# First attention: 32-row scores in two row groups, values of two units in four column groups of one bank, the inputs of the values behind the first scores

## The reference, cut to what matters

```python
qkv = x @ qkv_w + qkv_b                       # 8 heads of 8 channels
attn = einsum('bijnd,bijnpqd->bijnpq', q * hd**-0.5, kn) + bias   # a 7x7 neighbourhood
a = softmax(attn)
out = einsum('bijnpq,bijnpqd->bijnd', a, vn) @ proj_w + proj_b
gate = sigmoid(relu(x @ g1_w + g1_b) @ g2_w + g2_b)
y = x + out * gate                            # then a layer norm
```

## Time and profile before

| | us |
|---|---|
| median of 3 runs | 428.79 (427.92 to 429.21) |
| profiled execution | 428.27 |
| its span, first to last instruction | 426.5 |
| PE busy in the span | 292.1 (68%) |
| DVE busy | 258.1 (61%) |
| ACT busy | 212.3 (50%) |
| first attention: from the first scores to the end of the last values | 10.95 to 42.2 |

### The profile page before, as it was taken

The page is one execution under the profiler, slowest core; times in us unless marked ns, Lnnn a source line. Parts: engine busy times, 40 slices in busy tenths (PEclk is TensorE's granted clock), DMA queues, the critical chain, the costliest instruction groups (busy, mean ns, idle before and its releaser), DMA issues.

```text
span 426.5 us, 11844 instructions
## 1 busy us (share of the span) xinstructions
PE 292.1 (68%) x3273; PEld 224.0 (53%) x3278; DVE 258.1 (61%) x2308; ACT 212.3 (50%) x1172; POOL 12.2 (3%) x22
## 2 busy tenths in 40 slices
PE   6899889989866666665566666655666666556663
PEld 3466348642555555555555555555555555555552
DVE  1785454655456666666666666666666666666665
ACT  2787262253645555555555555555555555555552
POOL 5320000000000000000000000000000000000000
PEclk9999998899965555555555555555555555555555
DMA  7500000000000000000000000000000000000000
GB/s 277 222 3 2 0 2 1 0 2 0 1 2 2 0 0 0 0 0 0 0 0 0 0 0 0 0 0 0 0 0 0 0 0 0 0 0 0 0 0 12
DMA packets 2972, 5.60 MB, mean 13 GB/s; under 512 B 1424, under 2 KB 1680, under 8 KB 2960
## 3 DMA queue, kind: packets, MB, share of 16 engines
q1 hardware_dynamic: 2672, 5.09, 3.2%
q10 hardware_dynamic: 288, 0.36, 0.2%
HBM read 5.32 MB, written 0.13 MB: 13 GB/s over the span
## 4 chain that ended last, share of the span: by engine, by line
ACT 39%; PE 38%; DVE 14%; issue 8%; DMA 1%; SPq 0%; ACTq 0%; DVEq 0%
PE bank L665 18%; ACT bank L383 17%; ACT go L377 10%; ACT gi L371 8%; DVE ha L949 6%; DVE terms_a L949 4%; PE bank L424 2%; PE bank L446 2%; PE bank L394 2%; PE bank L435 1%; PE bank L597 1%; PE bank L558 1%; PE bank L609 1%; DMA cst<-in_const 1%; PE bank L479 1%
## 5 line engine op out<-in xcount | busy, mean ns | idle before, releaser
L665 PE MATMUL bank<-ha,vparts 128*128 128x1 f16 x1536 | 95.5, 169 | 117.5 <-DVE ha L949 117.5
L665 PEld LDWEIGHTS bank<-ha,vparts 128*128 128x128 f16 x1536 | 74.7, 106 | 140.3 <-DVE ha L949 140.3
L371 ACT ACTIVATE gi<-bank 128x1 f32<-128x1 f32 x256 | 43.8, 171 | 151.7 <-PE bank L665 151.7
L383 ACT ACTIVATE bank<-bank,hc,gi 128x2 f32<-128x2 f32 x256 | 83.4, 326 | 0.0
L946 DVE TENSOR_SCALAR go<-go 128x1 f32<-128x1 f32 x256 | 39.3, 154 | 72.2 <-ACT go L377 72.2
L665 PE MATMUL bank<-hb,vparts 128*128 128x1 f16 x768 | 69.5, 165 | 0.0
L949 DVE CUSTOM_DVE_ANT_0 terms_a<-bank,go 128x3 f32<-128x3 f32 x256 | 41.1, 161 | 29.5 <-ACT bank L383 0.2
L661 PE MATMUL bank<-x,w5s 128*128 (+1 forms) x198 | 56.0, 358 | 0.1
L474 PE MATMUL bank<-ones,w5s 128*128 128x8 f32 x198 | 55.7, 356 | 0.0
L955 DVE SCALAR_TENSOR_TENSOR cell<-bank,gi,hc 128x1 f32<-128x1 f32 x256 | 54.7, 214 | 0.0
L665 PEld LDWEIGHTS bank<-hb,vparts 128*128 128x128 f16 x768 | 53.9, 104 | 0.0
(11 more groups left out here) (215 smaller groups left out, 293.8 us busy)
## 6 DMA issues: line engine op xcount, KB each, us to landing
rel<-in_positions SPq DMA_DIRECT2D x4, 352.0 KB, 6.7
w3s<-in_w SPq DMA_DIRECT2D x1, 804.0 KB, 10.5
ltr<-in_later SPq DMA_DIRECT2D x1, 709.0 KB, 8.6
w2s<-in_w SPq DMA_DIRECT2D x1, 640.0 KB, 9.6
w5s<-in_w SPq DMA_DIRECT2D x1, 576.0 KB, 11.4
w0s<-in_w ACTq DMA_DIRECT2D x1, 336.0 KB, 4.0
w1s<-in_w SPq DMA_DIRECT2D x1, 256.0 KB, 8.8
w4s<-in_w SPq DMA_DIRECT2D x1, 192.0 KB, 11.3
```

The lines of the kernel that those rows point to most:

```text
L371: act.activation(gi[:], bank[pre + 1][:, at:at + 1], ACT.Sigmoid, scale=1.0 / PRE)
L383: act.activation(tc_ends, gt.broadcast_to([P, 2]), ACT.Tanh, scale=gi[:], bias=hc[:]).then_inc(on("tanh_c"), 1)
L665: return mm(bank[3 * parity + k][:, at:at + 1], vparts[:, part, k], h, start=False, stop=False, skip_group_check=True)
```

## The change

Head `pair` h now means heads `pair` and `pair + 4`: one lies in the first 32 channels of its image, one in the second 32. The keys are kept four times instead of eight (`km`, heads taken modulo 32 channels), and the queries once, without zeros: a product takes the 32 partitions of one image and one half of the heads as its rows (`r`), so that its rows alone select image and half. Scores are issued for two units at once, as four products of 176 columns that alternate between two row groups and two banks. Values are issued for two units at once, as eight products that go round four column groups of one bank, first all of the first half of the keys, then the second. The four products for the values' inputs and the gate's second product are issued behind the first scores. `gateh` on ACT goes behind the second pair of exponentials. The blank products at the start are nine instead of five, with one more behind the turns of the input. POOL no longer zeroes `q0`. The order of units is now: half of the heads, query half, image, and the two pairs of a half innermost, so that units 0 and 1 need the tables of pairs 0 and 1.

```diff
-WARM_UP = 5
+WARM_UP = 9
-        q0 = sb("q0", [P, B, N])
-        km = sb("km", [P, HEADS, N])
+        q0 = sb("q0", [P, N])
+        km = sb("km", [P, HEADS // 2, N])
-        pt = sb("pt", [KCH, 3, 4, P])
+        pt = sb("pt", [KCH, 4, 4, P])
-        UNITS = [(b, qt, pair) for pair in range(HEADS // 2) for qt in range(HALVES) for b in range(B)]
-        PER_PAIR = HALVES * B
+        UNITS = [(b, qt, 2 * half + j) for half in range(2) for qt in range(HALVES) for b in range(B) for j in range(2)]
+        PER_HALF = NU // 4
-            pool.memset(q0[:], 0.0).then_inc(on("q0_zero"), 1)
...
-            for b in range(B):
-                r = slice(b * C, (b + 1) * C)
-                act.activation(q0[r, b], bank[0][r, 0:N], ACT.Identity, scale=HD ** -0.5,
-                               bias=bq0s[r]).then_inc(on("q0"), 1)
+            act.activation(q0[:], bank[0][:, 0:N], ACT.Identity, scale=HD ** -0.5,
+                           bias=bq0s[:]).then_inc(on("q0"), 1)
...
+                if u == 1:
+                    act.wait_ge(on("g2_mm"), 1)
+                    act.wait_ge(on("g2bh"), 1)
+                    act.activation(gateh[:], bank[7][:, 0:N], ACT.Tanh, bias=g2bh[:], scale=0.5)\
+                       .then_inc(on("gateh"), 1)
...
+            keep_clock(bank[1], 1)
             pe.wait_ge(on("xf"), 1)
...
-            def scores(u):
-                b, qt, pair = UNITS[u]
-                if u >= 4:
-                    pe.wait_ge(on("neg_max"), 2 * (u - 3))
-                mm(bank[u % 4][:, 0:2 * KEYS], q0[:, b, qt * P:(qt + 1) * P],
-                   km[:, 2 * pair:2 * pair + 2, at:at + KEYS], start=True, stop=True).then_inc(on("s_mm"), 1)
+            def scores(s):
+                b, qt, first = UNITS[2 * s]
+                if s >= 2:
+                    pe.wait_ge(on("neg_max"), 4 * (s - 1))
+                for j in range(2):
+                    for h in range(2):
+                        r = slice((2 * b + h) * ROWS, (2 * b + h + 1) * ROWS)
+                        m = mm(bank[2 * (s % 2) + h][:, j * KEYS:(j + 1) * KEYS], q0[r, qt * P:(qt + 1) * P],
+                               km[r, first + j, at:at + KEYS], start=True, stop=True)
+                m.then_inc(on("s_mm"), 1)
...
+            def values(s):
+                pe.wait_ge(on("pt_ready"), 2 * s + 2)
+                for ch in range(2):
+                    for u in (2 * s, 2 * s + 1):
+                        b, qt, pair = UNITS[u]
+                        g, j = divmod(pair, 2)
+                        for h in range(2):
+                            row = 32 * (2 * j + h)
+                            m = mm(bank[6 + g][row:row + 32, (b * HALVES + qt) * P:(b * HALVES + qt + 1) * P],
+                                   vch[:, 2 * qt + ch, b * HEADS + HEADS // 2 * h + pair], pt[:, u % 4, 2 * h + ch],
+                                   start=(ch == 0), stop=(ch == 1), skip_group_check=True)
+                m.then_inc(on("pv_mm"), 1)
-            pe.wait_ge(on("q0"), B)
-            for u in range(NU + 5):
-                if u < NU:
-                    scores(u)
+            pe.wait_ge(on("q0"), 1)
+            for u in range(NU + 4):
+                if u < NU and u % 2 == 0:
+                    scores(u // 2)
+                if u == 0:
+                    inputs_of_values()
                 if 3 <= u < NU + 3:
                     turn(u - 3)
-                if u >= 5:
-                    values(u - 5)
+                if u >= 6 and u % 2 == 0:
+                    values(u // 2 - 3)
+            values(NU // 2 - 1)
...
-                if u % PER_PAIR < 2 and u // PER_PAIR < HEADS // 2 - 1:
-                    if u == 0:
+                if u in (2, 4):
+                    if u == 2:
                         dve.wait_ge(on("k0"), 1)
-                    masked_k(2 * (u // PER_PAIR) + 2 + u % PER_PAIR)
+                    masked_k(2 + u // 4)
```

More of the change, by code:

```diff
@@ L274, in _ @@
             act.activation(vch[:, :, :, 0:HD].rearrange("p a h d -> p (a h) d"),
[L275 to L278, removed]
+                           bank[6][0:KCH, :].rearrange("p (a d) -> p a d", d=HD), ACT.Copy).then_inc(on("vch"), 1)
             def numerators(u):
@@ L292, in turned_copy @@
                 act.wait_ge(on("p_turned"), u + 1)
-                if u >= 3:
-                    act.wait_ge(on("pv_mm"), u - 2)
-                act.activation(pt[:, u % 3].rearrange("p a c -> p (a c)"), bank[4 + u % 2][0:KCH, :], ACT.Copy)\
+                if u >= 4 and u % 2 == 0:
+                    act.wait_ge(on("pv_mm"), u // 2 - 1)
+                act.activation(pt[:, u % 4].rearrange("p a c -> p (a c)"), bank[4 + u % 2][0:KCH, :], ACT.Copy)\
                    .then_inc(on("pt_ready"), 1)
@@ L407, in _ @@
             mm(bank[0][:, 0:N], cols(w0s, W0, "q"), xf[:], start=True, stop=True).then_inc(on("q0_mm"), 1)
[L408 to L413, removed]
@@ L415, in scores @@
-            def scores(u):
-                b, qt, pair = UNITS[u]
-                at = KROW0[qt] * SIDE
-                if u >= 4:
-                    pe.wait_ge(on("neg_max"), 2 * (u - 3))
[L420 to L423, removed]
-                mm(bank[u % 4][:, 0:2 * KEYS], q0[:, b, qt * P:(qt + 1) * P],
-                   km[:, 2 * pair:2 * pair + 2, at:at + KEYS], start=True, stop=True).then_inc(on("s_mm"), 1)
+            mm(bank[7][0:32, N:2 * N], cols(w0s, W0, "g1"), xf[:], start=True, stop=True).then_inc(on("g1_mm"), 1)
@@ new lines, in inputs_of_values @@
+            def inputs_of_values():
+                for qt in range(HALVES):
+                    for ch in range(2):
+                        at = KROW0[qt] * SIDE + ch * KCH
+                        mm(bank[6][0:KCH, (2 * qt + ch) * P:(2 * qt + ch + 1) * P], xf[:, at:at + KCH],
+                           cols(w0s, W0, "v"), start=True, stop=True).then_inc(on("v0_mm"), 1)
+                pe.wait_ge(on("g1_ready"), 1)
+                mm(bank[7][:, 0:N], cols(w0s, W0, "g2")[0:32], g1[:], start=True, stop=True).then_inc(on("g2_mm"), 1)
@@ L437, in turn @@
                 m.then_inc(on("p_turned"), 1)
[L439 to L448, removed]
-                m.then_inc(on("pv_mm"), 1)
-            pe.wait_ge(on("q0"), B)
-            for u in range(NU + 5):
-                if u < NU:
-                    scores(u)
-                if u == 1:
-                    pe.wait_ge(on("g1_ready"), 1)
-                    mm(bank[7][:, 0:N], cols(w0s, W0, "g2")[0:32], g1[:], start=True, stop=True).then_inc(on("g2_mm"), 1)
+            def values(s):
+                pe.wait_ge(on("pt_ready"), 2 * s + 2)
+                if s == 0:
+                    pe.wait_ge(on("vch"), 1)
+                for ch in range(2):
+                    for u in (2 * s, 2 * s + 1):
[6 more added lines that the diff above has]
+                                   start=(ch == 0), stop=(ch == 1), skip_group_check=True)
+                m.then_inc(on("pv_mm"), 1)
+            pe.wait_ge(on("q0"), 1)
[4 more added lines that the diff above has]
+                    inputs_of_values()
                 if 3 <= u < NU + 3:
                     turn(u - 3)
-                if u == 5 + NU // 2:
+                if u == 6:
                     pe.wait_ge(on("gateh"), 1)
-                if u >= 5:
-                    values(u - 5)
+                if u >= 6 and u % 2 == 0:
+                    values(u // 2 - 3)
+            values(NU // 2 - 1)
             keep_clock(bank[4], 3)
@@ L1012, in both, with spread @@
         return rows(np.tile(x.reshape(-1, 1), (2, 1)))
-    def spread(x):
-        x = x.reshape(4, HD, -1)
+    def spread(x, half):
+        heads = [2 * half + j + HEADS // 2 * h for j in range(2) for h in range(2)]
+        x = x.reshape(HEADS, HD, -1)[heads]
         return np.pad(x, ((0, 0), (0, 32 - HD), (0, 0))).reshape(P, -1)
@@ L1051 @@
     vec = {n: both(x) for n, x in vec.items()} | {f"b1_{e}": a["L2_ffn_b1"][e].reshape(HID, 1) for e in range(E)}
-    vec |= {f"bv0_{g}": spread(qb[2 * C + g * C // 2:2 * C + (g + 1) * C // 2]) for g in range(2)}
+    vec |= {f"bv0_{g}": spread(qb[2 * C:], g) for g in range(2)}
     vec["gateb"] = np.tile(a["L2_ffn_gate_b"].reshape(1, E), (P, 1))
```

25 lines of the change are left out of this document (14 added, 11 removed).

## The result

The changed kernel takes 428.91 us (median of 20 runs, 428.39 to 431.83) where the kernel before has 428.21 (20 runs, 427.73 to 429.21). The ratio of the runs is 1.0023 (that of the two medians is 1.0016), 95% interval 1.0014 to 1.0033: 0.23% slower, within what was called no change. The forecast was 422.4 with a range of 420.4 to 426.3. The profiled execution of the changed kernel has a span of 427.7 us (429.5 of device time), 1.2 more than before.

A forecast was written before the change was run, and what follows sets the result against it. PE was taken as the bound at 1.79 us a unit, ACT next at 1.36. Front 2.2, units 0 to 15 3.6 and tail 0.7 sum to 6.5 less, on the median 428.8 - 6.4 = 422.4 us, range 420.4 to 426.3.

The forecast's parts named there:

- what was called no change: Whole kernel: a measured time within about 0.3%, 1.3 us, of the kernel before; chance 0.06.
- What bounds the kernel: Steady attention: PE bounds at 1.79 us a unit, then ACT 1.36, DVE 1.17; at most 0.44 a unit to gain.
- PE's price of a pair at full pace: Steady attention: scores 0.79, turns 1.12, values 0.59 us, together 2.50 for two units, below ACT's 1.36 a unit.
- The front: Start up to the first exponential: clock rises at 7.2, first exponential at 11.17 instead of 13.34, 2.2 us earlier.
- the rival of the late clock: Front: the clock rises as late as before, gain 0.8 us instead of 2.2, time 423.8; chance 0.13.
- Units 0 to 15 and the tail: First to last exponential pair 20.5 us instead of 24.1; then to bank 7's copy 4.1 instead of 4.8.
- The rival with the fallen clock: Attention: PE's clock falls, 2.4 us a unit at half pace; 432.9 us with ten such units; chance 0.07 for 430 and more.
- What happens later: Behind the attention: everything starts earlier, not shortened; half clock from 72 to 78.8 may move, taken as 0, 1.5 either way.
- the rival of no change: Whole kernel: pairing makes ACT wait for PE as now, front hangs on something else, within 1.3 us of 428.8; chance 0.06.

The follow-up runs named there:

- the kernel with the burst: The changed kernel plus one burst of 14 blank products of 512 columns ahead of the scores of units 8 and 9: 426.81 us, ratio 0.9962.
- the gaps filled: The changed kernel plus blank products where PE waits, ten ahead of the turn of unit 0, five ahead of that of unit 2: 421.98 us, ratio 0.9831.

## Why the prediction was wrong, point by point

- **What bounds the kernel:** right. PE was the bound, and ACT is next: with the clock held, ACT waits for 0.3 us in eleven units and its exponentials stand 1.33 a unit apart from 24.96 to 31.60, where 1.36 was forecast. (Over all fifteen steps, the slower first ones included, it is 20.6 / 15 = 1.37.)
- **PE's price of a pair at full pace:** forecast 2.50 (1.25 a unit), measured 2.51 in the kernel with the burst. Row groups and four column groups run side by side in full; with two groups forecast 3.05, measured 3.07. The estimate from the figure for three column groups in the Trainium skill (TensorE: Matmul & The Clock Gate, Measured speedup vs the span model), 1.31 a unit, would have been too high; the values of two units take 0.57, no more than the 0.59 forecast for four groups in full.
- **The front:** forecast 2.2 earlier with a rise at 7.2, bound 2.8 with a rise at 5.4. Measured 2.7 with the rise at 4.9 in the changed kernel, but only 0.7 in the profiled execution with the gaps filled, where the clock rose at 10.2: the rival of the late clock. Missed in it: POOL's cast now falls on the first scalings and stretches them by 0.8 us. It counted as starting by its DMA and costing nothing; what it runs beside was not asked.
- **Units 0 to 15 and the tail:** forecast 20.5 and 4.1, measured 20.6 and 4.1 with the gaps filled, but 29.2 and 5.0 in the changed kernel.
- **The step that failed** is the assumption under the whole sum that the clock, once up, stays. In the sum this term stands at nothing. The laid-out schedule itself has PE's values' inputs end at 10.5, and the turn of unit 0 behind a normalising that ends at 12.8 (11.2 + 0.98 + 0.64), with little more than one pair's scores between; PE's empty time was in it and was never priced. In place of a clock that stays, the granted clock was 0.50 from 15.2 to 42.4. Its price in the attention is 34.2 us from the first exponential to the copy of bank 7 against 24.6 with the gaps filled (44.77 - 10.59 and 37.28 - 12.63): 9.5 us. Between the medians, 428.91 and 421.98, it is 6.9; the profiled execution of the filled kernel had its clock up only at 10.2 and its first exponential 2.0 later than the changed kernel. That the fall came with the waits of the first units is shown by filling them; what the narrow scores add to it is open.
- **The rival with the fallen clock** named the mechanism and the engine, but gave it 0.07 and the wrong time, 430 and more. It priced 2.4 a unit, measured 2.26: its three terms as printed give 1.39 + 1.98 + 1.06 = 4.43 a pair, near the measured 4.51, and what it added for the changes was too much. It took the clock to be lost in the steady pairs, where it was lost in the first units; in the steady pairs it was only not regained. The evidence held against it, PE busy 5.77 of 7 us before the change, was of the very products that the change shortens: 128-row scores filled that stretch.
- **What happens later:** taken as no change, with 1.5 either way. In the profiled executions it was 1.9 the good way, but nothing ties that to the change. What counts is how long the half clock lasts there. From the copy of bank 7 to the recurrence the fourteen traces have 75.8 to 76.3 us where it lasts 6.8 us (eight of them, the kernel before and the changed kernel with the cast moved among them), 74.1 to 74.6 where it lasts 3.4 (five, the changed kernel and the kernel before with nine blank products among them), and 73.5 where there is none (the run with five blank products, 45.31 to 118.81).
- **The range** left out 428.9 because 0.06 stood for no change and 0.07 for slower, as two separate cases. They met: a gain of about the forecast size, and a loss that took it away. So the time came out where the rival of no change had it, but by luck: that rival's mechanism, units tied together by the pairing, is not what happened.

## What to carry to other kernels

Where a change makes TensorE's work shorter, look for the places where it will now stand idle, at the start of a pipeline above all, and price the clock there as a term of the sum. A clock lost at the start may not come back while the loop runs (here 0.50 from 15.2 to 42.4): check in the profile whether it does, and try blank products in the gap. Blank products all through the loop came out about as well here (422.45 against 421.98, intervals that overlap). And when a stage starts earlier, list what the other engines do at that time, POOL's copies beside VectorE's scalings too.

## What the runs showed of the hardware that was not expected

- The same mix of 32-row, 32-column and transposing products keeps a full clock up for over 14 us (22.7 to 37.0, PE busy 13.4 of 14.3) and does not raise a half one from 15.2 on (PE busy 25.7 of 27.2 us). Which property of the products decides was not tried, but the traces point at the 32-row scores: in the four in which the half clock lasted through the attention it came back, without a blank product, only behind the last scores (scores over at 37.2, 36.8, 36.3 and 37.5, rise at 42.4, 40.5, 42.7 and 43.3, in the changed kernel and the runs with the values' order undone, the cast moved and five blank products).
- In the six traces in which the clock fell in the first units it did so at 12.4 to 16.0, while PE waited or soon behind a wait (in the changed kernel at 15.1, the wait having ended at 13.2). A wait of 0.89 was followed by a fall with 32-row scores (13.1, two blank products with each pair); waits of 0.80 and 0.85 in the kernel before, and of 1.10 and 1.25 in the run with 128-row scores, were not.
- The order in which products of different column groups are issued did not matter, as long as no wait stood between them: unit by unit (1.03) or interleaved (1.01), sixteen records take the same time at half pace up to the next step. Interleaved at full pace they take 0.57 (26.69 to 27.26), no more than eight records did.
- Two scalings of DVE beside a cast of POOL took 1.35 us instead of 0.53; with the cast moved away, the same two took 0.53.
